# Residual vector quantizer: three index searches a unit over up to seven score tiles, in place of five

## The chip, the cores and the metric

One Trainium2 chip, one core of it. The metric is the device time of the whole kernel in microseconds (us): before the change 1495.66, the median of three runs (1492.65 to 1497.45).

## The reference

Four blocks run one after the other on x of shape (16, 32, 32, 32), each adding its result to x: a residual vector quantizer (L0), a frequency-domain attention block (L1), a directional scan network (L2) and a deformable convolution (L3). The change is in L0 alone:

```python
def _L0_conv_ref(embeddings, codebooks):      # 16384 pixels of 32 channels, 8 codebooks of 512 codes
    x = embeddings.transpose(0, 2, 3, 1).reshape(-1, e)
    def stage(res, cb):
        d = sum(res * res) - 2.0 * einsum('ne,ke->nk', res, cb) + sum(cb * cb)
        idx = argmin(d, axis=1)
        q = cb[idx]
        return (res - q, q)
    _, qs = scan(stage, x, codebooks)
    return sum(qs)
...
x = x + _L0_conv_ref(_gn(x), L0_conv_codebooks)
```

For every pixel and each of eight stages the nearest of 512 codes is found and subtracted from what is left of the pixel.

## The kernel before, in words

**Units.** `block_l0` holds the residual in SBUF as eight pieces `res[:, i, :]`, each of 128 partitions (4 images x 32 channels) by 512 pixels. One piece at one stage is a unit; eight stages make `ALL` = 64 units, in one software pipeline: unit w is scored in period w, its indices are turned into one-hot vectors in period w + 2, its codes are picked in w + 3, and so on (`back(w, n)` names the unit n periods back). A piece comes back for its next stage eight periods later.

**Tiles and slots.** A unit has 16 score tiles: 4 images (row groups of 32 partitions) by 4 runs of 128 pixels. A period has five slots of 4, 3, 4, 3, 2 tiles (even units) or 3, 4, 3, 4, 2 (odd ones), written out in `PLANS`. The slots use two areas of PSUM in turn (four banks and three). Before the change tile n is row group n // 4 and pixel run n % 4, and a slot takes every fourth number, so that its tiles lie in different row groups.

**Scores.** The codes are paired, so a tile's 512 columns are 256 sums and 256 differences. For a slot, TensorE makes the tiles (`scores`, L293 with the code norms and L298 in float32), ScalarE takes the relu of the difference half into `gain` (L423), and VectorE adds the sum half and the gain, scales by 4096 to the power of the tile's place, keeps the result in `scored` and its maximum in `top` (L669; each is followed in the trace by a read of the accumulator). TensorE may write slot k only when the tops of slot k - 2 are there, the area's last user.

**Search.** `find` (L637) looks up the positions of up to eight `top` values in the scored tiles of a slot. In the trace it is a load of the values (MATCH_VALUE_LOAD) and FIND_INDEX8. It stands one slot behind its scores, behind the pair sums of the next slot: the search of slot 0 behind slot 1, and so on, that of slot 4 behind slot 0 of the next unit. The low byte of a position is the pair's number in its tile.

**Order on VectorE** (`period`): slot 0, search of the last unit's slot 4; slot 1, transpose of the last unit's indices (`turn`, L646), search of slot 0; slot 2, the middle of the picked pair subtracted from the residual of unit w - 3 (`add_middle`, L652), search of slot 1; slot 3, search of slot 2; slot 4, search of slot 3. Ahead of each slot's pair sums stand two waits, each with a semaphore increment behind it: for the tops of the slot before, and for ScalarE's gain.

**Index rows.** SyncE writes the transposed indices to DRAM with one DMA (L238), waits for it, and reads them back, broadcast to all partitions, into `ib` (L243); it also loads each stage's codes and codebooks behind these (L220, L224, L225). GpSimd makes the near one-hots from `ib` (L515, four a unit), ScalarE the far ones in two steps (L398, L404).

**Picks.** TensorE multiplies the one-hots by the codebook (`pick`, L306): behind slots 0 and 1 the step, which ScalarE copies (L433), behind slots 2 and 3 the middle, which `add_middle` takes. Behind slot 4 comes one product matmul (L351), which waits for `add_middle` of the same period; ScalarE takes its sign (L449), and GpSimd updates the residual (L525, L535) and makes the next product (L543).

Of the kernel before, what the change touches and what calls it, by code (L numbers as in the profile page):

```python
# [46 lines left out]
    ((0, (0, 4, 8, 12)), (1, (1, 5, 9)), (0, (2, 6, 10, 14)), (1, (7, 11, 15)), (0, (3, 13))),  # L47
    ((1, (4, 8, 12)), (0, (1, 5, 9, 13)), (1, (2, 6, 10)), (0, (3, 7, 11, 15)), (1, (0, 14))),
)
SLOTS = 5  # L50
WIDE = 4
FOUND = 104
# [10 lines left out]
def block_l0(nc, ps, X, io, const, w1, next1):  # L63
# [14 lines left out]
    scratch = nc.dram_tensor("l0_indices", (2, TT, 2 * TILES, C), U16, kind="Internal").ap()  # L78
    with ExitStack() as ctx:
# [32 lines left out]
        scored = t("scored", [P, 3, WIDE * PAIRED])  # L112
        top = t("top", [P, 2, SLOTS, 8])
        idx = t("idx", [P, 2, FOUND], U16)
        turned = t("turned", [P, 2, 2 * TILES], U16)
        ib = t("ib", [P, 2, TT, TILES * C], U16)
# [5 lines left out]
        codes = scored[:, 0:1, :].rearrange("p o (s k) -> p (o s) k", k=K)  # L122
# [59 lines left out]
        def low(par, g, n):  # L182

            halves = ib[:, par].bitcast(U8).rearrange("p b (s c two) -> p s b c two", c=C, two=2)
            return halves[:, TT * g:TT * (g + n), :, :, 0]

        def spread(tile):

            return tile.rearrange("p (s b c) -> p s b c", b=TT, c=C)
# [12 lines left out]
        def _(sp):  # L202
# [30 lines left out]
            for v in range(ALL):  # L233
# [4 lines left out]
                sp.dma_start(scratch[par].rearrange("b s c -> (b s) c"), turned[:, par, :]).then_inc(s_wrote[par], 16)  # L238
                sp.wait_ge(s_wrote[par], START + 16 * (v // 2 + 1))
                if v >= 2:  # L240
# [3 lines left out]
                             scratch[par, :, 0:TILES, :].rearrange("b s c -> b (s c)").partition_broadcast(P)  # L244
# [17 lines left out]
        def _(pe):  # L262
# [18 lines left out]
            def scores(w, k):  # L281
# [9 lines left out]
                for m, n in enumerate(tiles):  # L291
                    rows = slice(C * (n // TT), C * (n // TT) + C)
                    pe.matmul(ps[:, at + m, :], row_slot[rows, par, :], csq[rows, :],  # L293
                              start=True, stop=False, skip_group_check=True)
                for m, n in enumerate(tiles):
                    rows = slice(C * (n // TT), C * (n // TT) + C)
                    tt = n % TT
# [62 lines left out]
        def _(act):  # L360
# [35 lines left out]
            def distance(v, g):  # L396

                nc.scalar.activation(spread(away[:, g:g + 2, :].rearrange("p g n -> p (g n)")), low(v % 2, g, 2),  # L398
# [156 lines left out]
        def _(dve):  # L555
# [74 lines left out]
            def find(w, k):  # L630

                area, tiles = PLANS[w % 2][k]
                at = (SLOTS * w + k) % 3
                if SLOTS * w + k:
                    dve.wait_ge(s_found, START + SLOTS * w + k)
                base, by = tiles[0], tiles[1] - tiles[0]
                nc.vector.max_index(idx[:, w % 2, base:base + 7 * by + 1:by],  # L637
                                    top[:, w % 2, k, :],
                                    scored[:, at, 0:len(tiles) * PAIRED]).then_inc(s_found, 1)

            def turn(v):

                dve.wait_ge(s_found, START + SLOTS * (v + 1))
                if v >= 2:
                    dve.wait_ge(s_wrote[v % 2], START + 16 * (v // 2))
# [8 lines left out]
            def period(w):  # L654

                early, mid = back(w, 1), back(w, 3)
                for k in range(SLOTS):
# [10 lines left out]
                    for m in range(len(tiles)):  # L668
                        nc.vector.tensor_tensor_reduce(  # L669
                            out=scored[:, (SLOTS * w + k) % 3, m * PAIRED:(m + 1) * PAIRED],  # L670
                            in0=ps[:, at + m, :PAIRED], in1=gain[:, at + m, :], scale=STEP_UP ** m, scalar=LOWEST,
                            op0=ALU.add, op1=ALU.max, accum_out=top[:, w % 2, k, m:m + 1]).then_inc(s_top, 1)
                    if k == 0 and early is not None:
                        find(early, SLOTS - 1)
                    if k == 1 and early is not None:
                        turn(early)
                    if k == 2 and mid is not None:
# [1536 lines left out]
```

## Time and profile before

| | before |
|---|---|
| median of three runs | 1495.66 us (1492.65 to 1497.45) |
| the profiled execution, its own time | 1497.99 us |
| its span, first to last instruction | 1495.9 us |
| busy over the span | PE 82%, DVE 78%, ACT 58%, POOL 64% |
| quantizer: first and last transposed indices | 41.1 us and 759.9 us |

PE is TensorE, DVE VectorE, ACT ScalarE, POOL GpSimd, SPq SyncE's DMA queue. In timeline rows the columns are the start from the span's start, the duration, the engine, the line of the kernel, the operation, output<-input and form, how many, and in brackets the engine's idle time before it and what ended it. An operation's row ends when its last result is written; the next one on the same engine can begin before that.

### The profile page before, as it was taken

Reading aid. Unit: us, or ns where it says so; the run is one execution under the profiler, and the core shown is the slowest. Engines: PE = TensorE matmul, PEld = TensorE weight load, DVE = VectorE, ACT = ScalarE, POOL = GpSimd, SP = SyncE. Lnnn points to the kernel's source line nnn. Section 1 sums busy time; section 2 is a strip of 40 time slices with the busy share of each in tenths; the row PEclk is TensorE's granted clock in tenths of the full one; section 3 lists DMA queues with packets and bytes.
Section 4 is the critical chain, followed back from the end, with each engine's and each line's share of the span. In section 5 each row is a group of like instructions: output and inputs, shape, how many; then the busy total and the mean of one; then the engine's idle time right before and its main releaser. Section 6 shows DMA issues by size and latency. Waiting matters only on the chain. (4 is left out here: it accounts for less than half of the span.)

```text
span 1495.9 us, 30285 instructions
## 1 busy us (share of the span) xinstructions
PE 1229.4 (82%) x10814; PEld 505.9 (34%) x10814; DVE 1170.9 (78%) x3667; ACT 871.4 (58%) x1169; POOL 954.5 (64%) x727
## 2 busy tenths in 40 slices
PE   4798988988988988988968899958888667776675
PEld 1222222222222222222215666626656411121111
DVE  6999999999999999999976455562222358887886
ACT  2687888888888888888843444320000046676654
POOL 5699888888888898898820332321000059989885
PEclk7799999999999999999979999989999959889877
DMA  7111211111121111111104433410000030202001
GB/s 175 52 44 44 68 46 55 45 52 60 45 68 45 53 48 57 55 44 58 44 30 101 106 89 86 103 41 18 2 1 2 23 73 1 48 1 62 1 15 29
DMA packets 65894, 74.43 MB, mean 50 GB/s; under 512 B 17776, under 2 KB 55920, under 8 KB 65744
## 3 DMA queue, kind: packets, MB, share of 16 engines
q1 hardware_dynamic: 64544, 70.68, 17.3%
q10 hardware_dynamic: 1200, 1.82, 0.5%
q8 instruction: 86, 1.41, 0.4%
q14 instruction: 64, 0.52, 0.1%
HBM read 42.21 MB, written 2.62 MB: 30 GB/s over the span
## 5 line engine op out<-in xcount | busy, mean ns | idle before, releaser
L515 POOL TENSOR_SCALAR l_onehot<-l_ib,c_cols 128x512 bf16<-128x512 uint8 x248 | 385.1, 1565 | 9.6 <-DMA l_ib<-l_indices 9.6
L669 DVE CUSTOM_DVE_ANT_0 l_scored<-ps,l_gain 128x256 f32<-128x256 f32 x1024 | 373.5, 416 | 14.2 <-ACT l_gain L423 13.4
L423 ACT ACTIVATE l_gain<-ps 128x1024 f32<-128x1024 f32 (+1 forms) x320 | 272.6, 852 | 144.9 <-PE ps L298 144.8
L298 PE MATMUL ps<-l_ct_slot,l_res 32*128 32x512 f32 x2048 | 340.1, 607 | 0.0
L637 DVE FIND_INDEX8 l_idx<-l_top,l_scored 128x8 uint16<-128x1024 f32 (+1 forms) x320 | 326.4, 1020 | 0.0
L1896 POOL TENSOR_TENSOR l_isum<-l_term 128x512 f32<-128x512 f32 x160 | 204.8, 1311 | 40.2 <-DVE l_term L2000 25.9
L306 PE MATMUL ps<-l_onehot,l_cbp_slot 128*32 128x512 bf16 x3072 | 217.1, 391 | 5.9 <-ACT l_signed L449 3.1
L293 PE MATMUL ps<-l_csq,l_row_slot 32*128 32x512 bf16 x1024 | 128.7, 394 | 84.0 <-DVE l_top L669 78.8
L1626 PE MATMUL ps<-l_isum,w_l_w_dsc 64*64 64x512 f32 x640 | 104.4, 713 | 59.8 <-POOL l_isum L1896 58.8
L1816 ACT ACTIVATE ps<-ps,w_l_minus 128x512 f32<-128x512 f32 x192 | 118.6, 661 | 51.2 <-DVE l_term L2006 35.1
L398 ACT ACTIVATE l_away<-l_ib,c_cols 128x1024 f16<-128x1024 uint8 x126 | 143.8, 1141 | 0.4 <-DMA l_ib<-l_indices 0.4
L404 ACT ACTIVATE l_onehot<-l_away,c_cols 128x1024 bf16<-128x1024 f16 x126 | 143.6, 1139 | 0.1
L306 PEld LDWEIGHTS ps<-l_onehot,l_cbp_slot 128*32 128x32 bf16 x3072 | 60.0, 96 | 230.2 <-issue 147.5
L298 PEld LDWEIGHTS ps<-l_ct_slot,l_res 32*128 32x128 f32 x2048 | 130.2, 191 | 7.4 <-issue 0.7
L2006 DVE SCALAR_TENSOR_TENSOR l_term<-ps,l_bend 128x512 f32<-128x512 f32 x192 | 120.7, 681 | 14.4 <-ACT ps L1816 12.8
L293 PEld LDWEIGHTS ps<-l_csq,l_row_slot 32*128 32x128 bf16 x1024 | 33.3, 91 | 263.7 <-DVE l_top L669 155.6
L1863 POOL COPY l_xe<-l_xe 128x128 f32<-128x128 f32 (+1 forms) x16 | 4.5, 308 | 183.9 <-DVE l_xe L1913 183.6
L525 POOL TENSOR_TENSOR l_signed<-l_signed,l_step 128x512 f32<-128x512 f32 x59 | 75.4, 1277 | 68.7 <-ACT l_signed L449 67.9
L2000 DVE SCALAR_TENSOR_TENSOR l_term<-ps,l_down 128x512 f32<-128x512 f32 x128 | 80.1, 680 | 26.0 <-PE ps L1618 15.8
L943 PE MATMUL ps<-l_wc,l_xi 128*128 128x192 f32 x512 | 93.0, 335 | 0.3 <-ACT l_qkv L1031 0.3
L943 PEld LDWEIGHTS ps<-l_wc,l_xi 128*128 128x128 f32 x512 | 83.6, 192 | 25.8 <-issue 17.1
L543 POOL TENSOR_TENSOR l_product<-l_res,l_step 128x512 f32<-128x512 f32 x61 | 77.8, 1275 | 12.6 <-DVE l_res L652 12.6
(214 smaller groups left out, 1604.3 us busy)
## 6 DMA issues: line engine op xcount, KB each, us to landing
l_ib<-l_indices SPq DMA_DIRECT2D x64, 512.0 KB, 3.7
l_xi<-l_xt SPq DMA_DIRECT2D x120, 128.0 KB
l_xi<-l_xz SPq DMA_DIRECT2D x36, 144.2 KB, 3.1
X<-in_x SPq DMA_DIRECT2D x16, 128.0 KB, 6.6
out<-X SPq DMA_DIRECT2D x16, 128.0 KB, 2.2
l_xr<-l_xt SPq DMA_DIRECT2D x30, 64.0 KB
l_ct<-in_codes_t SPq DMA_DIRECT2D x4, 448.0 KB, 12.1
l_ct_slot<-l_ct SPq DMA_DIRECT2D x7, 256.0 KB, 3.7
```

The costliest lines, as they stand in the source:

```text
L293: pe.matmul(ps[:, at + m, :], row_slot[rows, par, :], csq[rows, :], start=True, stop=False, skip_group_check=True)
L298: pe.matmul(ps[:, at + m, :], res[rows, i, P * tt:P * (tt + 1)], ct_slot[rows, par, :], start=False, stop=True, skip_group_check=True).the ...
L306: mm = pe.matmul(ps[C * g:C * g + C, PICK, :], cbp_slot[:, v // UNITS % 2, kind, a, c, :], onehot[:, v % 2, g, c, :], start=(c == 0 and a ...
L398: nc.scalar.activation(spread(away[:, g:g + 2, :].rearrange("p g n -> p (g n)")), low(v % 2, g, 2), ACT.Abs, bias=minus_iota[:, 1:2]).then ...
L404: nc.scalar.activation(onehot[:, v % 2, g:g + 2, 1, :], away[:, g:g + 2, :], ACT.Relu, bias=one[:], scale=-1.0).then_inc(s_far, 1)
L423: nc.scalar.activation(gain[:, at:at + len(tiles), :], ps[:, at:at + len(tiles), PAIRED:], ACT.Relu).then_inc(s_gain, 1)
L515: nc.gpsimd.tensor_scalar(spread(onehot[:, v % 2, g, 0, :]), low(v % 2, g, 1), iota[:, 0:1], None, ALU.is_equal).then_inc(s_near, 1)
L637: nc.vector.max_index(idx[:, w % 2, base:base + 7 * by + 1:by], top[:, w % 2, k, :], scored[:, at, 0:len(tiles) * PAIRED]).then_inc(s_foun ...
L669: nc.vector.tensor_tensor_reduce(out=scored[:, (SLOTS * w + k) % 3, m * PAIRED:(m + 1) * PAIRED], in0=ps[:, at + m, :PAIRED], in1=gain[:, ...
L943: pe.matmul(ps[:, CONV_BANKS[py % 2] + u, 0:HID], xi[:, n, g, at:at + P], wc[:, n, :], start=(n == 0), stop=False)
L1896: nc.gpsimd.tensor_tensor(isum[:, it % SUMS, :], term[:, t0, :], term[:, t0 + 1, :], ALU.add).then_inc(s_sum, 1)
L2006: nc.vector.scalar_tensor_tensor(out=dst, in0=grid(ps[:, RAMP + (p * NR + RAMP_OF[2 * n + e]) % RAMPS, :]), scalar=1.0, in1=bend[:, j % 2, ...
```

## The change

The tiles are numbered pixel run by pixel run, row group fastest (tile n is now row group n % 4 and pixel run n // 4), and a slot takes consecutive numbers. A search now covers the tiles of two slots: tiles 0 to 6, 7 to 13, and 14 and 15. `scored` gets a place for each of the three, `top` likewise. On VectorE the search of tiles 0 to 6 stands behind the pair sums of slot 2 and ahead of `add_middle`, that of tiles 7 to 13 behind slot 4, that of 14 and 15 behind slot 0 of the next unit. Behind slot 1 stands the transpose alone, behind slot 3 nothing. The DRAM rows of the indices are laid out so that a broadcast read is one run of 4 KB for each partition; to get there the transposed indices are written by four DMAs of 16 partitions.

```diff
--- before.py
+++ after.py
@@ -44,12 +44,12 @@
 SPAN = 2 * (2 / 1024 + 1 / 8192)
 
 PLANS = (
-    ((0, (0, 4, 8, 12)), (1, (1, 5, 9)), (0, (2, 6, 10, 14)), (1, (7, 11, 15)), (0, (3, 13))),
-    ((1, (4, 8, 12)), (0, (1, 5, 9, 13)), (1, (2, 6, 10)), (0, (3, 7, 11, 15)), (1, (0, 14))),
+    ((0, (0, 1, 2, 3)), (1, (4, 5, 6)), (0, (7, 8, 9, 10)), (1, (11, 12, 13)), (0, (14, 15))),
+    ((1, (0, 1, 2)), (0, (3, 4, 5, 6)), (1, (7, 8, 9)), (0, (10, 11, 12, 13)), (1, (14, 15))),
 )
 SLOTS = 5
-WIDE = 4
-FOUND = 104
+WIDE = 7
+SEARCHES = 3
 END = [[sum(len(plan[m][1]) for m in range(k + 1)) for k in range(SLOTS)] for plan in PLANS]
 KEPT = 4
 DRAIN = 5
@@ -75,7 +75,7 @@
     iota, eps = const["iota"], const["eps"]
     minus_iota, one, block_ones = const["minus_iota"], const["one"], const["block_ones"]
     part_mask, kept_rows, shift_row = const["part_mask"], const["kept_rows"], const["shift_row"]
-    scratch = nc.dram_tensor("l0_indices", (2, TT, 2 * TILES, C), U16, kind="Internal").ap()
+    scratch = nc.dram_tensor("l0_indices", (2, TILES, TT, C), U16, kind="Internal").ap()
     with ExitStack() as ctx:
         def t(name, shape, dt=F32):
             return ctx.enter_context(nc.sbuf_tensor("l0_" + name, shape, dt))
@@ -109,17 +109,17 @@
         cbp = t("cbp", [P, NC, 2, PARTS, CHUNKS, C], BF16)
         cbp_slot = t("cbp_slot", [P, 2, 2, PARTS, CHUNKS, C], BF16)
         gain = t("gain", [P, PICK, PAIRED])
-        scored = t("scored", [P, 3, WIDE * PAIRED])
-        top = t("top", [P, 2, SLOTS, 8])
-        idx = t("idx", [P, 2, FOUND], U16)
+        scored = t("scored", [P, SEARCHES, WIDE * PAIRED])
+        top = t("top", [P, 2, SEARCHES, 8])
+        idx = t("idx", [P, 2, 2 * TILES], U16)
         turned = t("turned", [P, 2, 2 * TILES], U16)
-        ib = t("ib", [P, 2, TT, TILES * C], U16)
+        ib = t("ib", [P, 2, TILES * P], U16)
         away = t("away", [P, G, HALF], F16)
         onehot = t("onehot", [P, 2, G, CHUNKS, HALF], BF16)
         step = t("step", [P, KEPT, HALF])
         product = t("product", [P, 2, HALF])
         signed = t("signed", [P, HALF])
-        codes = scored[:, 0:1, :].rearrange("p o (s k) -> p (o s) k", k=K)
+        codes = scored[:, 0, 0:2 * K].rearrange("p (s k) -> p s k", k=K)
 
         s_x = [sem(f"x{j}") for j in range(J)]
         s_codes = sem("codes")
@@ -181,12 +181,12 @@
 
         def low(par, g, n):
 
-            halves = ib[:, par].bitcast(U8).rearrange("p b (s c two) -> p s b c two", c=C, two=2)
-            return halves[:, TT * g:TT * (g + n), :, :, 0]
+            halves = ib[:, par].bitcast(U8).rearrange("p (t g n two) -> p g t n two", g=G, n=P, two=2)
+            return halves[:, g:g + n, :, :, 0] if n > 1 else halves[:, g, :, :, 0]
 
         def spread(tile):
 
-            return tile.rearrange("p (s b c) -> p s b c", b=TT, c=C)
+            return tile.rearrange("p (t n) -> p t n", n=P)
 
         def ib_ready(v):
 
@@ -235,13 +235,14 @@
                 sp.wait_ge(s_turned, START + v + 1)
                 if v >= 2:
                     sp.wait_ge(s_ib[par], ib_ready(v - 2))
-                sp.dma_start(scratch[par].rearrange("b s c -> (b s) c"), turned[:, par, :]).then_inc(s_wrote[par], 16)
-                sp.wait_ge(s_wrote[par], START + 16 * (v // 2 + 1))
+                for b in range(TT):
+                    sp.dma_start(scratch[par, :, b, :], turned[C * b:C * b + TILES, par, :]).then_inc(s_wrote[par], 16)
+                sp.wait_ge(s_wrote[par], START + 16 * TT * (v // 2 + 1))
                 if v >= 2:
                     sp.wait_ge(s_near, START + G * (v - 1))
                     sp.wait_ge(s_far, far_ready(v - 2))
                 sp.dma_start(ib[:, par],
-                             scratch[par, :, 0:TILES, :].rearrange("b s c -> b (s c)").partition_broadcast(P)
+                             scratch[par].rearrange("s b c -> (s b c)").partition_broadcast(P)
                              ).then_inc(s_ib[par], 16)
                 if v % UNITS == 1 and stage < NC:
                     sp.wait_ge(s_diff, START + 2 * stage)
@@ -289,12 +290,12 @@
                 elif w:
                     pe.wait_ge(s_top, START + (w - 1) * TILES + END[(w - 1) % 2][k + SLOTS - 2])
                 for m, n in enumerate(tiles):
-                    rows = slice(C * (n // TT), C * (n // TT) + C)
+                    rows = slice(C * (n % G), C * (n % G) + C)
                     pe.matmul(ps[:, at + m, :], row_slot[rows, par, :], csq[rows, :],
                               start=True, stop=False, skip_group_check=True)
                 for m, n in enumerate(tiles):
-                    rows = slice(C * (n // TT), C * (n // TT) + C)
-                    tt = n % TT
+                    rows = slice(C * (n % G), C * (n % G) + C)
+                    tt = n // G
                     pe.matmul(ps[:, at + m, :], res[rows, i, P * tt:P * (tt + 1)],
                               ct_slot[rows, par, :],
                               start=False, stop=True, skip_group_check=True).then_inc(s_score, 1)
@@ -627,22 +628,19 @@
             dve.wait_ge(s_clear, START + 2)
             dve.wait_ge(s_sums, START + 1)
 
-            def find(w, k):
-
-                area, tiles = PLANS[w % 2][k]
-                at = (SLOTS * w + k) % 3
-                if SLOTS * w + k:
-                    dve.wait_ge(s_found, START + SLOTS * w + k)
-                base, by = tiles[0], tiles[1] - tiles[0]
-                nc.vector.max_index(idx[:, w % 2, base:base + 7 * by + 1:by],
-                                    top[:, w % 2, k, :],
-                                    scored[:, at, 0:len(tiles) * PAIRED]).then_inc(s_found, 1)
+            def find(w, n):
+
+                first, last = WIDE * n, min(WIDE * (n + 1), TILES)
+                if SEARCHES * w + n:
+                    dve.wait_ge(s_found, START + SEARCHES * w + n)
+                nc.vector.max_index(idx[:, w % 2, first:first + 8], top[:, w % 2, n, :],
+                                    scored[:, n, 0:(last - first) * PAIRED]).then_inc(s_found, 1)
 
             def turn(v):
 
-                dve.wait_ge(s_found, START + SLOTS * (v + 1))
+                dve.wait_ge(s_found, START + SEARCHES * (v + 1))
                 if v >= 2:
-                    dve.wait_ge(s_wrote[v % 2], START + 16 * (v // 2))
+                    dve.wait_ge(s_wrote[v % 2], START + 16 * TT * (v // 2))
                 nc.vector.transpose(turned[:, v % 2, :], idx[:, v % 2, 0:2 * TILES]).then_inc(s_turned, 1)
 
             def add_middle(v):
@@ -665,19 +663,22 @@
                         dve.sem_inc(s_alone, 1)
                     dve.wait_ge(s_gain, START + w * SLOTS + (k + 1))
                     dve.sem_inc(s_alone, 1)
-                    for m in range(len(tiles)):
+                    for m, n in enumerate(tiles):
+                        search, place = divmod(n, WIDE)
                         nc.vector.tensor_tensor_reduce(
-                            out=scored[:, (SLOTS * w + k) % 3, m * PAIRED:(m + 1) * PAIRED],
-                            in0=ps[:, at + m, :PAIRED], in1=gain[:, at + m, :], scale=STEP_UP ** m, scalar=LOWEST,
-                            op0=ALU.add, op1=ALU.max, accum_out=top[:, w % 2, k, m:m + 1]).then_inc(s_top, 1)
+                            out=scored[:, search, place * PAIRED:(place + 1) * PAIRED],
+                            in0=ps[:, at + m, :PAIRED], in1=gain[:, at + m, :], scale=STEP_UP ** place, scalar=LOWEST,
+                            op0=ALU.add, op1=ALU.max, accum_out=top[:, w % 2, search, place:place + 1]).then_inc(s_top, 1)
                     if k == 0 and early is not None:
-                        find(early, SLOTS - 1)
+                        find(early, 2)
                     if k == 1 and early is not None:
                         turn(early)
+                    if k == 2:
+                        find(w, 0)
                     if k == 2 and mid is not None:
                         add_middle(mid)
-                    if k:
-                        find(w, k - 1)
+                    if k == 4:
+                        find(w, 1)
                     if w < 2:
                         late_quarters(w, k)
 
@@ -725,7 +726,7 @@
                 if early is not None:
                     dve.wait_ge(s_top, START + early * TILES + TILES)
                     dve.sem_inc(s_alone, 1)
-                    find(early, SLOTS - 1)
+                    find(early, 2)
                     turn(early)
                 if i == 0:
                     for e in range(UNITS - DRAIN):
```

## Rows read from the trace of the kernel before

**Rows 1.** Busy time by stretch: us, each engine's busy time (instructions), TensorE's granted clock, DMA.

```profile
0.00:100.00 100.00, 71.04 (x481) 23.04 (x481) 82.86 (x294) 55.55 (x77) 65.29 (x67) 0.80 0.37 96
418.58:429.70 11.12, 10.21 (x100) 3.27 (x98) 11.12 (x45) 9.28 (x12) 9.18 (x8) 1.00 0.26 76
429.70:441.27 11.57, 10.23 (x105) 3.27 (x98) 11.33 (x46) 9.34 (x12) 10.71 (x8) 1.00 0.21 57
```

**Rows 2.** The page's groups by line: busy us, mean ns | idle before, what ended it.

```profile
L669 DVE CUSTOM_DVE_ANT_0 l_scored<-ps,l_gain 128x256 f32<-128x256 f32 x1024 | 373.5, 416 | 14.2 <-ACT l_gain L423 13.4
```

**Rows 3.** Timeline of VectorE, an even unit (four tiles in slot 0).

```profile
418.58 0.42 DVE L669 CUSTOM_DVE_ANT_0 l_scored<-ps,l_gain 128x256 f32<-128x256 f32 x1
...
419.96 0.08 DVE L669 DVE_READ_ACCUMULATOR2_ANT l_top<- 128x1 f32 x1
419.96 0.09 DVE L637 MATCH_VALUE_LOAD l_idx<-l_top,l_scored 128x8 f32 x1
...
420.64 0.40 DVE L669 CUSTOM_DVE_ANT_0 l_scored<-ps,l_gain 128x256 f32<-128x256 f32 x1
...
422.96 0.41 DVE L669 CUSTOM_DVE_ANT_0 l_scored<-ps,l_gain 128x256 f32<-128x256 f32 x1
...
424.32 0.68 DVE L652 TENSOR_TENSOR l_res<-l_res,ps 128x512 f32<-128x512 f32 x1
...
425.86 0.40 DVE L669 CUSTOM_DVE_ANT_0 l_scored<-ps,l_gain 128x256 f32<-128x256 f32 x1
...
426.88 0.08 DVE L637 MATCH_VALUE_LOAD l_idx<-l_top,l_scored 128x8 f32 x1
...
428.09 0.40 DVE L669 CUSTOM_DVE_ANT_0 l_scored<-ps,l_gain 128x256 f32<-128x256 f32 x1
```

**Rows 4.** Timeline of VectorE, the odd unit behind it, to the next one's start.

```profile
429.70 0.40 DVE L669 CUSTOM_DVE_ANT_0 l_scored<-ps,l_gain 128x256 f32<-128x256 f32 x1
...
431.67 0.42 DVE L669 CUSTOM_DVE_ANT_0 l_scored<-ps,l_gain 128x256 f32<-128x256 f32 x1 [0.16 <-ACT l_gain L423]
...
434.09 0.40 DVE L669 CUSTOM_DVE_ANT_0 l_scored<-ps,l_gain 128x256 f32<-128x256 f32 x1
...
441.27 0.42 DVE L669 CUSTOM_DVE_ANT_0 l_scored<-ps,l_gain 128x256 f32<-128x256 f32 x1
```

**Rows 5.** Timeline of TensorE, the same two units.

```profile
420.10 0.39 PE L293 MATMUL ps<-l_csq,l_row_slot 32*128 32x512 bf16 x4 [0.16 <-DVE l_top L669]
...
425.64 1.12 PE L351 MATMUL ps<-l_product,c_block_ones 128*128 128x512 f32 x2
427.10 0.39 PE L293 MATMUL ps<-l_csq,l_row_slot 32*128 32x512 bf16 x3 [0.34 <-DVE l_top L669]
...
431.00 0.39 PE L293 MATMUL ps<-l_csq,l_row_slot 32*128 32x512 bf16 x3
```

**Rows 6.** Timeline of ScalarE, the same two units.

```profile
421.50 1.02 ACT L423 ACTIVATE l_gain<-ps 128x1024 f32<-128x1024 f32 x1 [0.90 <-PE ps L298]
...
430.46 1.02 ACT L423 ACTIVATE l_gain<-ps 128x1024 f32<-128x1024 f32 x1 [0.15 <-PE ps L298]
...
432.36 0.81 ACT L423 ACTIVATE l_gain<-ps 128x768 f32<-128x768 f32 x1 [0.41 <-PE ps L298]
```

**Rows 7.** Timeline of VectorE in the first unit, a slot behind a short instruction.

```profile
35.23 0.42 DVE L669 CUSTOM_DVE_ANT_0 l_scored<-ps,l_gain 128x256 f32<-128x256 f32 x1 [0.33 <-DVE l_rstd L569]
```

**Rows 8.** Timeline of SyncE's DMA issues, the same units.

```profile
421.89 0.32 SPq L238 DMA_DIRECT2D l_indices<-l_turned  x1
423.30 0.37 SPq L243 DMA_DIRECT2D l_ib<-l_indices  x1
423.76 0.47 SPq L224 DMA_DIRECT2D l_ct_slot<-l_ct  x1
```

**Rows 9.** The page's DMA issues: KB each, median us to landing.

```profile
l_ib<-l_indices SPq DMA_DIRECT2D x64, 512.0 KB, 3.7
```

**Rows 10.** Timeline of GpSimd, the odd unit's first near one-hot.

```profile
429.43 1.57 POOL L515 TENSOR_SCALAR l_onehot<-l_ib,c_cols 128x512 bf16<-128x512 uint8 x1
```

More of the change, by code:

```diff
@@ L396, in distance @@
             def distance(v, g):
-                nc.scalar.activation(spread(away[:, g:g + 2, :].rearrange("p g n -> p (g n)")), low(v % 2, g, 2),
+                nc.scalar.activation(away[:, g:g + 2, :].rearrange("p g (t n) -> p g t n", n=P), low(v % 2, g, 2),
                                      ACT.Abs, bias=minus_iota[:, 1:2]).then_inc(s_away, 1)
```

## The prediction

> **What bounds the kernel now.** I read the busy time by stretch first. Two successive units of the quantizer, taken at 418.58 us, last 11.12 and 11.57 us, 22.69 together, and VectorE is busy for 22.45 of them; TensorE has 20.44, GpSimd 19.89 and ScalarE 18.62 [rows 1]. So VectorE is the bound here. The groups by line say the same: before 1024 pair sums VectorE sat idle for only 14.2 us, nearly all of it until a relu of ScalarE was done [rows 2]. An edit on VectorE therefore counts at full price, as long as the next scores are ready when VectorE gets to them. That second half is what the timelines are for. I call the moments at which slots 0 to 4 of a unit start on VectorE T0 to T4.
>
> In the first unit shown (an even one: four tiles in slot 0) they are 418.58, 420.64, 422.96, 425.86 and 428.09 [rows 3]; the next unit starts at 429.70, with its T1 at 431.67, T2 at 434.09 and its end at 441.27 [rows 4]. Out of these come the unit prices. A pair sum takes 0.345 (four from 418.58 to 419.96), and its top stands 0.08 after the last. A search with its load takes 0.68 over 512 elements (419.96 to 420.64) and 1.21 over 1024 (426.88 to 428.09) [rows 3]: 0.265 per 256 elements and 0.15 that does not grow with them.
>
> **Term 1, the searches.** Five a unit (1024, 1024, 768, 768, 512) become three (1792, 1792, 512). The 4096 elements stay. By the line above 768 costs 0.945 and 1792 costs 1.21 + 3 x 0.265 = 2.00. Before: 2 x 1.21 + 2 x 0.945 + 0.68 = 4.99; after 4.68. Gain 0.31 a unit. No search of 1792 is in the trace; from slope errors of 0.01 it lies between 1.96 and 2.04.
>
> **Term 2, the handover of slot 2.** The two PSUM areas are used in turn, so the scores of slot k wait for the tops of slot k - 2. From T0 on, TensorE starts the four tiles of slot 2 1.52 later (420.10) [rows 5], ScalarE ends their relu 2.42 after that (421.50 + 1.02) [rows 6], and the shortest way from a relu's end to VectorE's start is 0.19 (430.46 + 1.02 = 431.48 to 431.67) [rows 4, 6]. So T2 cannot come before T0 + 4.13. It came at + 4.38: the cover was 0.25. That cover was the search of slot 0, 1.21 long, which stood behind slot 1. The change takes it away and puts its successor behind slot 2. VectorE is then free at T0 + 3.2 and waits: T2 = T0 + 4.13. Moving a search does not only move its cost, it uncovers a wait.
>
> **Term 3, VectorE waits for itself.** Before slot 4 there is no longer any work between the last pair sum of slot 3 and the wait for its top. Each such wait is followed by a semaphore increment, another wait and another increment. The nearest row is a slot that had to wait for a short VectorE instruction: 0.33 of idle time [rows 7]. I take 0.33 behind the last top, so 0.41 with the 0.08; the other bound is 0. In odd units slot 1's four tops also meet this wait, behind the transpose. A page of the Trainium skill speaks for the 0 (VectorE: DVE Perf Modes, The DRAIN you can't avoid): eight copies took the same time with a semaphore after each as with one at the end. By that the sum would be 1519; the row of this kernel shows 0.33 and decides my value.
>
> **The walk.** Even unit, from 418.58. T1 stays 420.64. T2 = 422.71. T3: before, 2.90 with a search of 0.945; now 2.90 - 0.945 + 2.00 = 3.955, so 426.67. T4: 2.23 - 1.21 + 0.41 = 1.43, so 428.10. End: 1.61 - 0.945 + 2.00 = 2.665, so 430.77 against 429.70. The middle's add now starts at 422.71 + 1.36 + 2.00 = 426.07 and ends 0.68 later at 426.75 (its 1.36 and 0.68 from [rows 3]). TensorE's product matmul waits for it, takes 1.12 [rows 5], and the next unit's scores start behind it at about 427.95. Their data would be ready by 430.3, so the end stands at 430.77 with some 0.4 of cover: this is where the later add would bite next.
>
> Odd unit. T1: VectorE is free at 430.77 + 1.03 + 0.68 = 432.48; TensorE's own path needs 4.57 from the first scores (427.10 to 431.67 [rows 4, 5]), so 427.95 + 4.57 = 432.52. T2: four pair sums and the wait for itself, 432.52 + 1.38 + 0.41 = 434.31; the three tiles' handover ends at about the same time (TensorE free at 431.9, then 2.17 from 431.00 to 432.36 + 0.81, then 0.19 [rows 5, 6]: 434.26). T3: 1.02 + 2.00 + 0.60 = 3.62, so 437.93. T4: 1.36 + 0.41, so 439.70. End: 2.665, so 442.37 against 441.27.
>
> A pair of units takes 23.79 instead of 22.69: 1.10 more, 0.55 a unit. There are 64; counting 62 for fill and drain gives **+34 us**. The profiled execution took 1497.99 (span 1495.9), so 1532.1 for such a run; it lies 2.3 above the median of the runs shown, 1495.66, so against that median 1529.8. With 0 for term 3 the same walk gives 23.44 a pair, +23 us and 1519.
>
> **What I cost at nothing.** The new order of tiles keeps four different row groups in a slot of four, so the scores should stay side by side. Four writes of index rows instead of one: a write is issued in about 0.46 (423.30 to 423.76) and the read followed the write by 1.41 [rows 8]; the read lands 3.7 later, at 427.0 [rows 9], and GpSimd takes it up at 429.43 [rows 10]. Three more issues put that 1.4 later, inside the 2.4 of cover, and the longer unit adds to it. SP's next loads of codes and codebooks stand behind the same three issues and are wanted a unit later. If the cover were gone, GpSimd's one-hots would be late for the picks. GpSimd and ScalarE read the indices in fewer, longer runs; they are not the bound, so a gain there is worth nothing. In the first units TensorE's granted clock was lower (0.80 on average over the first 100 us against 1.00 in the units above [rows 1]); the slot 2 wait is longer there, a few us in all.
>
> **Rivals.**
> 1. *VectorE stays the bound and only the searches count* (not slower). For it: VectorE is busy 99% of the two units, and the searches have a cost of 0.15 each that does not grow. Gain 0.31 and some 0.06 of former waits a unit, 62 times: -23 us, **1473**. It decides if the path from TensorE's start to VectorE's start of slot 2, 2.61 by the rows, is below 1.7. Against it: every piece of that path is a measured duration and none is edited. Chance 0.13.
> 2. *Half-way*: the search over 1792 costs less than the line says. Each 0.1 less saves 0.2 a unit; 0.28 less and nothing is left, **about 1497**. Against it: the two steps of 256 elements cost the same. Chance 0.07.
> 3. *The index rows come late.* The four writes run one behind the other. By this kernel's 1.41 each they take 5.6, and rows land some 0.4 us into the next unit, 0.7 later than GpSimd asks for them; its 9.95 of work in a unit of 11.9 leaves 1.95 to absorb that. From some 2.5 us more (an estimate) it decides: the one-hots then miss the picks of slot 0, and since the way from one unit's indices to those picks spans two units, half of each further us is lost a unit. With 0.5 too much, +16 on top: **1546**. [...] Here one write took 1.41, and no row shows four in flight. Chance 0.05.
>
> **Numbers.** The forecast keeps 0.75. Under 0.3% (4.5 us) a measurement of this kernel cannot tell from no change. Faster by more: rival 1, 0.13. Within: 0.07. Slower: 0.80, the forecast and rival 3. The forecast's own bounds are 1516 (term 3 at 0, search 1.96) to 1536 (search 2.04, startup). The range reaches to both sides until at most 2 in 10 is out: down to 1502, up to 1546.
>
> **What would show it.** Slot 2 of even units starts with 0.7 to 1.0 us of idle time on VectorE that the trace puts down to the relu; a second, 0.2 to 0.4 long, stands before slot 4; a pair of units lasts 23.4 to 23.9; the search over 1792 reads about 2.03 long. VectorE's share falls to about 95% in this part, and everything behind the quantizer keeps its length. No idle time at slot 2 would mean that I am wrong and rival 1 right; GpSimd waiting for index rows would mean rival 3.

## The result, and the profile after

The changed kernel takes 1533.84 us (median of four runs, 1531.51 to 1537.49) against 1495.41 for the kernel before: the ratio on record is 1.0251, interval 1.0229 to 1.0273. The forecast was 1529.8 us in a range from 1502 to 1546, and slower with a chance of 0.80.

| | before | after |
|---|---|---|
| the profiled execution, its own time | 1497.99 us | 1531.51 us |
| its span | 1495.9 us | 1529.1 us |
| first to last transposed indices | 718.7 us | 757.7 us |
| from there to the end | 736.0 us | 730.1 us |

Lines of the code moved by one or two: the pair sums are L668 now, the search L636, the relu L424, the add of the middle L650, the product matmul L352, the index write L239 and its read L244.

Busy time by stretch of the changed kernel, an even unit and the odd one behind it (us, then busy time of PE, PEld, DVE, ACT and POOL, granted clock, DMA share, GB/s); it answers to [rows 1]:

```profile
363.73:375.94 12.21, 10.20 (x101) 3.24 (x98) 11.06 (x42) 9.38 (x12) 9.60 (x8) 1.00 0.12 45
375.94:387.55 11.61, 10.26 (x102) 3.28 (x98) 11.09 (x41) 9.43 (x12) 10.28 (x8) 1.00 0.14 46
```

A pair lasts 23.82 where it lasted 22.69. VectorE's busy time fell from 22.45 to 22.15, and it now sits idle for 1.67 us of the pair where it was 0.24. (The searches alone save 0.58 a pair, as shown below. The busy time falls by less, because a row overlaps the next by some 0.08 where no wait stands between them, and there are now four waits.) The other engines have the same work as before. Nothing was added to any of them; the time is waiting.

The timeline of VectorE over the same two units shows where; it answers to [rows 3, 4]:

```profile
363.73 0.41 DVE L668 CUSTOM_DVE_ANT_0 l_scored<-ps,l_gain 128x256 f32<-128x256 f32 x1
...
365.17 0.69 DVE L636 FIND_INDEX8 l_idx<-l_top,l_scored 128x8 uint16<-128x512 f32 x1
365.77 0.41 DVE L668 CUSTOM_DVE_ANT_0 l_scored<-ps,l_gain 128x256 f32<-128x256 f32 x1
...
366.79 0.21 DVE L644 STREAM_TRANSPOSE l_turned<-l_idx 128x32 uint16<-128x32 uint16 x1
367.85 0.42 DVE L668 CUSTOM_DVE_ANT_0 l_scored<-ps,l_gain 128x256 f32<-128x256 f32 x1 [0.85 <-ACT l_gain L424]
...
369.30 2.02 DVE L636 FIND_INDEX8 l_idx<-l_top,l_scored 128x8 uint16<-128x1792 f32 x1
371.24 0.67 DVE L650 TENSOR_TENSOR l_res<-l_res,ps 128x512 f32<-128x512 f32 x1
371.82 0.42 DVE L668 CUSTOM_DVE_ANT_0 l_scored<-ps,l_gain 128x256 f32<-128x256 f32 x1
...
373.24 0.42 DVE L668 CUSTOM_DVE_ANT_0 l_scored<-ps,l_gain 128x256 f32<-128x256 f32 x1 [0.30 <-DVE l_top L668]
...
375.94 0.41 DVE L668 CUSTOM_DVE_ANT_0 l_scored<-ps,l_gain 128x256 f32<-128x256 f32 x1
...
379.46 0.42 DVE L668 CUSTOM_DVE_ANT_0 l_scored<-ps,l_gain 128x256 f32<-128x256 f32 x1 [0.22 <-ACT l_gain L424]
...
384.85 0.42 DVE L668 CUSTOM_DVE_ANT_0 l_scored<-ps,l_gain 128x256 f32<-128x256 f32 x1 [0.30 <-DVE l_top L668]
```

Read it slot by slot. Behind slot 0 stands the short search, behind slot 1 the transpose alone, and then VectorE waits 0.85 us for the relu of slot 2's scores. Before slot 4 it waits 0.30 for its own last top, in both units. Slot 2 of the odd unit waits 0.22, by the trace for the relu.

The timeline of TensorE in the even unit:

```profile
365.23 0.40 PE L294 MATMUL ps<-l_csq,l_row_slot 32*128 32x512 bf16 x4 [0.40 <-DVE l_top L668]
...
369.60 1.02 PE L299 MATMUL ps<-l_ct_slot,l_res 32*128 32x512 f32 x4
372.05 1.10 PE L352 MATMUL ps<-l_product,c_block_ones 128*128 128x512 f32 x2 [1.43 <-DVE l_res L650]
373.08 0.39 PE L294 MATMUL ps<-l_csq,l_row_slot 32*128 32x512 bf16 x3
```

Slot 2's scores start at 365.23, as soon as slot 0's tops are there, and VectorE starts slot 2 at 367.85: 2.62, the same handover as before (2.61 from [rows 4, 5, 6]). And TensorE now idles 1.43 us before the product matmul, which waits for the later add. That did not lengthen this unit, but it comes back below.

### The profile page after: what moved, and what is told of

It is laid out like the page before. It is cut to its first block and busy times, and to the rows that moved or that the text cites. A ratio compares the mean times of both kernels' runs of the same rounds, so it can differ in the third digit from the quotient of the medians.

```text
span 1529.1 us, 30202 instructions
## 1 busy us (share of the span) xinstructions
PE 1218.9 (80%) x10795; PEld 505.3 (33%) x10814; DVE 1161.5 (76%) x3411; ACT 876.8 (57%) x1169; POOL 954.1 (62%) x727
## 5 line engine op out<-in xcount | busy, mean ns | idle before, releaser
L668 DVE CUSTOM_DVE_ANT_0 l_scored<-ps,l_gain 128x256 f32<-128x256 f32 x1024 | 376.7, 419 | 64.5 <-ACT l_gain L424 43.6
L424 ACT ACTIVATE l_gain<-ps 128x1024 f32<-128x1024 f32 (+1 forms) x320 | 271.9, 850 | 142.0 <-PE ps L299 137.8
L636 DVE FIND_INDEX8 l_idx<-l_top,l_scored 128x8 uint16<-128x1792 f32 (+1 forms) x192 | 302.5, 1576 | 0.0
L352 PE MATMUL ps<-l_product,c_block_ones 128*128 128x512 f32 x128 | 73.0, 653 | 80.2 <-DVE l_res L650 79.3
```

Source lines behind the costliest of these rows:

```text
L424: nc.scalar.activation(gain[:, at:at + len(tiles), :], ps[:, at:at + len(tiles), PAIRED:], ACT.Relu).then_inc(s_gain, 1)
L636: nc.vector.max_index(idx[:, w % 2, first:first + 8], top[:, w % 2, n, :], scored[:, n, 0:(last - first) * PAIRED]).then_inc(s_found, 1)
L668: nc.vector.tensor_tensor_reduce(out=scored[:, search, place * PAIRED:(place + 1) * PAIRED], in0=ps[:, at + m, :PAIRED], in1=gain[:, at + ...
```

## The experiments

Each ran on one chip beside the kernel before; its ratio is against those runs. Where units are given below, they are the time from one unit's transpose to the next one's: 11.29 and 11.40 in the kernel before, 11.58 and 12.24 in the changed one. Such a unit holds parts of an even and of an odd one, so the two numbers are not those of the stretches above; their sum is the same pair. Each profile is of one execution. The first five experiments ask which part of the change costs the time.

**1. The new layout alone.** The changed kernel with five searches again, one slot behind their scores:

```diff
-SEARCHES = 3
+SEARCHES = 5
...
-                    if k == 2:
-                        find(w, 0)
...
-                    if k == 4:
-                        find(w, 1)
+                    if k:
+                        find(w, k - 1)
```

> The changed kernel with five searches again, each one slot behind its scores as before; the new numbering of the tiles, the new layout of the index rows and the four DMA writes stay. My theory (the lost search between slots 1 and 2 and the waits of VectorE for itself make the loss): everything else in the change costs nothing, so 1495 us, within 5 of the kernel before, and a pair of units lasts 22.7 us. The rival that the rows or the layout cost the time: close to 1534, with GpSimd or ScalarE waiting for index rows.

Measured: 1494.19 us, 0.999 (0.997 to 1.0011), and units of 11.29 and 11.40 as before. The numbering of the tiles, the rows' layout, the four writes and the relative order of everything else cost nothing. The loss lies in the searches and where they stand.

**2. One write of index rows in the changed kernel.**

```diff
...
-                for b in range(TT):
-                    sp.dma_start(scratch[par, :, b, :], turned[C * b:C * b + TILES, par, :]).then_inc(s_wrote[par], 16)
...
+                sp.dma_start(scratch[par].rearrange("s b c -> b s c"), turned[:, par, :]).then_inc(s_wrote[par], 16)
...
```

> The changed kernel with one DMA for the index rows in place of four (the unused rows go along to their own place in DRAM; the read stays one run of 4 KB). Theory: the rows land earlier, nobody had waited for them, so 1534, within 4. Rival (four small writes cost time): 1500 to 1525.

The rows that hold no index go along, and `scratch` is twice as large for them.

Measured: 1530.83 us, 1.0232 (1.0198 to 1.0267), against 1.0251 (1.0229 to 1.0273) with four: no difference that these intervals resolve. SyncE's timeline in the changed kernel shows why four writes are no burden:

```profile
367.02 1.69 SPq L239 DMA_DIRECT2D l_indices<-l_turned  x4
369.72 0.34 SPq L244 DMA_DIRECT2D l_ib<-l_indices  x1
```

The read follows the first write by 2.70 where it was 1.41 [rows 8]: 1.3 later, 1.4 forecast. Four writes one behind the other, at 1.41 each, would have taken 5.6: the writes are in flight together.

**3. The cover put back.** The search of tiles 0 to 6 behind slot 1's transpose:

```diff
-                    if k == 2:
+                    if k == 1:
+                        dve.wait_ge(s_top, START + w * TILES + END[w % 2][1])
                         find(w, 0)
```

> The changed kernel with the search of tiles 0 to 6 moved from behind slot 2 to behind the transpose of slot 1, with a wait for its tops. Theory: the 0.9 us of idle time before slot 2 of even units goes, and slot 2 starts 5.2 us after the unit's start by the work in front of it. But the work between slots 2 and 4 is now only the add and slot 3, so a new wait for scores of about 0.6 stands before slot 4. A pair of units 23.3 instead of 23.8, time about 1520. Rival (the search is merely long and the place does not matter): 1534 unchanged.

Measured: 1530.47 us, 1.025 (1.0217 to 1.0284); not the 1520 expected. Most units last 11.27 and 12.08, 23.35 together as expected, and the idle time moved as expected. No slot 2 is idle any more. The rows with idle time in some two units of VectorE's timeline are a slot 1 of an odd unit that waits for its scores, slot 4 of the same unit that waits for its own top, and slot 4 of the even unit behind it, with the new wait for scores:

```profile
401.23 0.42 DVE L668 CUSTOM_DVE_ANT_0 l_scored<-ps,l_gain 128x256 f32<-128x256 f32 x1 [0.47 <-ACT l_gain L424]
...
408.12 0.42 DVE L668 CUSTOM_DVE_ANT_0 l_scored<-ps,l_gain 128x256 f32<-128x256 f32 x1 [0.30 <-DVE l_top L668]
...
419.62 0.42 DVE L668 CUSTOM_DVE_ANT_0 l_scored<-ps,l_gain 128x256 f32<-128x256 f32 x1 [0.53 <-ACT l_gain L424]
```

But about one in three of the long units lasts 13.45 instead of 12.08, ten in all, which makes some 14 us. TensorE's granted clock was at its lower level for 34 us of the quantizer in this profile. That needed an experiment of its own (6 and 7).

**4. The add first.** The middle's add ahead of the search again, everything else as changed:

```diff
-                    if k == 2:
-                        find(w, 0)
                     if k == 2 and mid is not None:
                         add_middle(mid)
+                    if k == 2:
+                        find(w, 0)
```

> The changed kernel with the add of the middle ahead of the search of tiles 0 to 6, as the order was before. Theory: the add then waits for TensorE's last middle pick, which stands behind the scores of slot 3; VectorE sits idle there for 0.8 to 1 us in units of both kinds, so a pair of units lasts 24.6 and the time is about 1560. So the move of the add is a part of the change that pays. Rival (the later add delays the product matmul and through it the next unit's scores, so that undoing it gains): under 1530.

Measured: 1611.12 us, 1.079 (1.0756 to 1.0824); some 50 above the 1560 expected. In stretches with the clock up a pair lasts 24.6, as expected (12.33 and 12.27), though not in the way expected: the add waits for TensorE's last pick in odd units only, 0.66 us in this row of VectorE's timeline. In even units, where slot 2 has waited 0.85 for its relu already, it does not wait:

```profile
170.63 0.69 DVE L650 TENSOR_TENSOR l_res<-l_res,ps 128x512 f32<-128x512 f32 x1 [0.66 <-PE ps L307]
```

So the move of the add pays, 0.8 us a pair. The further 50 us go with the clock again: 147 us at the lower level, and from the middle on pairs of 27.3. No experiment fills TensorE's idle time in this kernel, so that this is all of it is not shown.

**5. The waits moved to the searches.** No slot waits for the last slot's tops, each search waits for its own:

```diff
+                dve.sem_inc(s_alone, 1)
+                dve.wait_ge(s_top, START + w * TILES + last)
                 nc.vector.max_index(idx[:, w % 2, first:first + 8], top[:, w % 2, n, :],
...
-                    if k == 0 and early is not None:
-                        dve.wait_ge(s_top, START + early * TILES + TILES)
-                        dve.sem_inc(s_alone, 1)
-                    if k:
-                        dve.wait_ge(s_top, START + w * TILES + END[w % 2][k - 1])
-                        dve.sem_inc(s_alone, 1)
```

> The changed kernel without the wait for the last slot's tops ahead of each slot; each search waits for its own tops instead. Theory: the idle time of 0.3 before slot 4 goes in every unit. It is won fully in even units, in odd units part of it is given back at slot 1, which waits for its scores. A pair of units 23.4 instead of 23.8, time about 1522. Rival (a semaphore between VectorE instructions costs nothing, as a page of the Trainium skill has it): 1534 unchanged.

Measured: 1558.82 us, 1.0417 (1.0378 to 1.0455). Both expectations missed: the kernel became slower than the changed one. The pairs with the clock up did shrink, to 11.22 and 12.25, 23.47 together, 23.4 expected. But of every three long units one lasts 15.3 and one 13.8, and the clock was low for 95 us.

**6. TensorE's idle time filled.** Experiment 5, with four matmuls of 512 columns behind slot 4's scores, into a bank that nobody reads then. Their results are not used:

```diff
+FILL = 4
...
+                    if k == SLOTS - 1 and w < ALL and late is not None:
+                        area, tiles = PLANS[w % 2][k]
+                        spare = AREAS[area][0] + len(tiles)
+                        for _ in range(FILL):
+                            pe.matmul(ps[:, spare, :], row_slot[:, stage % 2, :], csq[:], start=True, stop=True,
+                                      skip_group_check=True)
```

> The kernel whose waits stand at the searches, plus four matmuls of 512 columns behind the scores of slot 4, into a PSUM bank that nobody reads then; they add no result and fill about 0.9 of the 2 us in which TensorE waits for the add. Theory: that kernel read 1559 instead of the 1522 expected, because TensorE's granted clock fell to its lower level for 96 us of the quantizer, and it fell because TensorE sat idle. With the gap partly filled it stays up, and what remains is the walk: a pair of units 23.5, time 1515 to 1525. Rival (the falls come from elsewhere, or the pair of units is longer for another reason): 1559 or more.

Measured: 1513.55 us, 1.0132 (1.01 to 1.0163), 1.5 below the 1515 to 1525 expected. More work on TensorE, and 45 us less. Busy time by stretch from 100 to 700 us, first without the filling (experiment 5), where the clock stands at 0.93:

```profile
100.00:700.00 600.00, 525.58 (x4715) 164.25 (x4716) 533.72 (x1925) 452.24 (x530) 484.49 (x344) 0.93 0.15 48
```

and with it, at 1.00:

```profile
100.00:700.00 600.00, 567.05 (x5215) 181.77 (x5211) 565.53 (x2041) 480.60 (x562) 515.13 (x366) 1.00 0.15 50
```

Nearly all units last 11.22 and 12.24, and from the fourth on none is over 12.4.

**7. The same filling in the changed kernel.**

> The changed kernel with the same four filling matmuls behind the scores of slot 4. Theory: the changed kernel's profile has TensorE at the lower clock for 10 us of the quantizer, which cost 5.3 us in two units; filled, it stays up, the pair of units stays at 23.8, time 1526 to 1530. Rival (the filling itself delays the scores of the next unit): a pair over 23.9 and 1534 or more.

Measured: 1528.8 us, 1.0208 (1.0185 to 1.0231), and its profile has units of 11.58 and 12.24 with no lower clock between the 85th us and the last transpose. The filling does not delay anything here: the pair is as long as without it. The gain against 1.0251 is small and the intervals just touch.

**8. The same filling in experiment 3.**

> The kernel with the search of tiles 0 to 6 behind slot 1, plus the four filling matmuls. Theory: its undisturbed pairs lasted 23.35, and the way from there to the measured 1530 was the clock, 34 us at the lower level in its profile; filled, 1513 to 1520. If the gap in which TensorE idles there is another one than the filled one, the clock still falls and 1530 stays.

Measured: 1545.77 us, 1.0329 (1.0305 to 1.0352): worse than without it, outside both expectations. The timeline of TensorE shows that the idle time lies ahead of slot 4's scores there, and the filling (L349) stands behind them, in the way of the next unit's scores. First experiment 3, then the same with the filling:

```profile
417.51 0.39 PE L294 MATMUL ps<-l_csq,l_row_slot 32*128 32x512 bf16 x2 [1.23 <-DVE l_top L668]
...
418.69 1.12 PE L352 MATMUL ps<-l_product,c_block_ones 128*128 128x512 f32 x2
419.75 0.39 PE L294 MATMUL ps<-l_csq,l_row_slot 32*128 32x512 bf16 x3
```

```profile
402.78 0.39 PE L295 MATMUL ps<-l_csq,l_row_slot 32*128 32x512 bf16 x2 [1.23 <-DVE l_top L675]
...
404.19 0.81 PE L349 MATMUL ps<-l_csq,l_row_slot 128*128 128x512 bf16 x3 [0.16 <-issue]
404.84 1.02 PE L359 MATMUL ps<-l_product,c_block_ones 128*128 128x512 f32 x2
405.79 0.39 PE L295 MATMUL ps<-l_csq,l_row_slot 32*128 32x512 bf16 x3
```

From slot 4's scores to the next unit's it is 3.01 where it was 2.24. The clock stayed up but for 3.4 us; the units became 11.99 and 12.59. Filling is no cure in itself: behind the gap it held the clock up here and cost more than that gave, in the gap (experiments 6 and 7) it cost nothing.

**9. Other groups.** Three searches, over slot 0, slots 1 and 2, and slots 3 and 4, at the changed kernel's places, with experiment 5's waits:

```diff
+GROUP = (0, 1, 1, 2, 2)
+RANGES = [[(end[0] - len(plan[0][1]), end[0]), (end[0], end[2]), (end[2], end[4])] for plan, end in zip(PLANS, END)]
...
-                first, last = WIDE * n, min(WIDE * (n + 1), TILES)
+                first, last = RANGES[w % 2][n]
...
-                        search, place = divmod(n, WIDE)
+                        search = GROUP[k]
+                        place = n - RANGES[w % 2][search][0]
```

> Three searches again, but over other slots: slot 0 alone, slots 1 and 2, slots 3 and 4, at the same places on VectorE as in the changed kernel (behind slot 2, behind slot 4, behind slot 0 of the next unit), and each search waits for its own tops instead of each slot for those of the last. Theory: the search behind slot 0 now covers 5 or 6 tiles and takes 1.5 to 1.7 us, so slot 2's scores are ready in time; no wait stands before slot 4. A pair of units takes 22.0 to 22.2 us against 22.69 before, so about 1476 us, under both kernels, and TensorE is so busy that its granted clock stays at its upper level. Rival (three searches a unit cost more than five by themselves): 1500 or more.

Measured: 1478.22 us, 0.9881 (0.9853 to 0.991), 1.2% faster than the kernel before. Units of 11.17 and 10.85. Its timeline of VectorE through slots 0 to 2 of an odd unit, and then of the even one behind it:

```profile
418.95 0.40 DVE L667 CUSTOM_DVE_ANT_0 l_scored<-ps,l_gain 128x256 f32<-128x256 f32 x1
...
420.04 1.49 DVE L640 FIND_INDEX8 l_idx<-l_top,l_scored 128x8 uint16<-128x1280 f32 x1
421.75 0.42 DVE L667 CUSTOM_DVE_ANT_0 l_scored<-ps,l_gain 128x256 f32<-128x256 f32 x1 [0.22 <-ACT l_gain L426]
...
423.14 0.21 DVE L648 STREAM_TRANSPOSE l_turned<-l_idx 128x32 uint16<-128x32 uint16 x1
423.27 0.38 DVE L667 CUSTOM_DVE_ANT_0 l_scored<-ps,l_gain 128x256 f32<-128x256 f32 x1
...
430.16 0.42 DVE L667 CUSTOM_DVE_ANT_0 l_scored<-ps,l_gain 128x256 f32<-128x256 f32 x1
...
431.62 1.75 DVE L640 FIND_INDEX8 l_idx<-l_top,l_scored 128x8 uint16<-128x1536 f32 x1
...
434.44 0.38 DVE L667 CUSTOM_DVE_ANT_0 l_scored<-ps,l_gain 128x256 f32<-128x256 f32 x1
```

The search behind slot 0 is 1.49 or 1.75 long instead of 0.69. In the odd unit slot 2 starts 0.13 behind the transpose's start. In the even unit, whose slot 2 had waited 0.85, it starts at +4.28, later than the +4.13 that the handover needs, and with no wait. The number of searches, their total length and the places are the changed kernel's, and the waits are experiment 5's; only which slots they cover differs.

**10. These groups with the changed kernel's waits.**

> The same three groups, but with the changed kernel's wait for the last slot's tops ahead of every slot. Theory: 0.3 to 0.4 us before slots 2 and 4 comes back, a pair of units takes 23.0, time about 1505, if the clock holds; more if it falls. Rival (own waits are free): the time of the kernel without them, 1476.

Measured: 1505.46 us, 1.007 (1.0044 to 1.0096), units of 11.53 and 11.53. The clock stayed up in the profiles of both. The waits for its own tops cost VectorE 27 us here by the two medians. Against the changed kernel, whose waits this one has, the grouping alone is worth 28 us (1505.46 against 1533.84).

**11. The control.** The kernel before, its waits moved to the searches:

> The kernel before with its waits for tops moved from the slots to the searches, nothing else. Theory: each of those waits was covered by the search that stood in front of it, so nothing changes, 1495 within 4; the gain of the regrouped kernel comes from the two searches fewer, not from this. Rival (the waits cost VectorE time there too): under 1488.

Measured: 1493.59 us, 0.998 (0.9965 to 0.9996), units of 11.29 and 11.40 as before. A gain of 0.2%, too small to matter: where a search stands in front of the wait, it costs nothing.

## Why the prediction was right

**The walk.** It gave an even unit of 12.19 and an odd one of 11.60, 23.79 together; the profile has 12.21 and 11.61, 23.82. Slots of the even unit were put at +2.06, +4.13, +8.09 and +9.52 and stand at +2.04, +4.12, +8.09 and +9.51. VectorE's share of this part was put at 95% and is 93%.

**Term 1.** The search over 1792 elements reads 2.02 long in the timeline, and load and search together take 2.01 from start to next start, 2.00 forecast. With 0.68 for the short one that makes 4.70 a unit instead of 4.99: 0.29 gained, 0.31 forecast, the saved fixed parts of two searches.

**Term 2.** The handover was forecast to place slot 2 at +4.13 and did. Experiment 9 shows the other half: with searches of the same number and sum, and a longer one behind slot 0, the wait is gone. Experiment 3 shows that putting the cover back at slot 2 uncovers slot 4: five gaps share two long searches, and which gap stays bare is what the grouping decides.

**Term 3.** 0.33 was taken, 0.30 measured before slot 4, in every unit. In slot 2 of the odd unit the walk had the wait for itself and the handover end within 0.05 of each other; by the trace it was the handover that ended last. With 0 for this term the walk gave 23.44 a pair, and experiment 5, without these waits, has 23.47. What it is worth was forecast as the step from 1519 to 1529.8, 11 us; experiments 6 and 7, which differ in these waits alone and both keep the clock, are 11 us apart by their ratios (0.0076 of 1495), 9.8 us in the profiles' quantizer (742.2 against 752.0), and 15 us by their medians, whose runs of the kernel before are 3 us apart too. In experiments 9 and 10 it is 27 us, where two slots a unit wait for themselves. The rule that I weighed against it (the Trainium skill, VectorE: DVE Perf Modes, The DRAIN you can't avoid: a semaphore after each of eight copies cost nothing extra) does not carry over to this wait: here a wait for a result, an increment, a second wait and a second increment stand between two instructions, and the trace shows 0.30 of idle time.

**What I costed at nothing** was nothing: experiments 1 and 2. The read of 4 KB runs still lands in 3.7 us. GpSimd waited for index rows once between the 100th and the 740th us, for 0.7 us. The first four intervals between transposes grew by 1.1 us in all, less than the walk alone gives for them (2.3), so the few us more that I had named for the lower clock there do not show. But up to the 85th us the clock was low for 41 us in the profile before and for 31 in the one after, so these two profiles do not settle it.

**The rest of the difference.** From first to last transpose the quantizer grew by 39.0 us, and 63 intervals at the pair's 0.565 each give 35.6. The first units took 1.1 us less than that. And the profile adds two stretches of lower clock that no step of mine contains, 4.6 us in two units (15.27 and 13.88, both instead of 12.24; the 5.3 in the expectation of experiment 7 compared the second with a short unit). Behind the quantizer 5.9 us came back. I had put that part at no change, and its code is the same; what differs is TensorE's clock, low there for 162 us in the profile before (0.89 on average) and for 129 in the one after (0.91):

```profile
759.86:1495.90 736.04, 565.96 (x4646) 293.26 (x4634) 436.16 (x822) 275.80 (x455) 307.57 (x249) 0.89 0.17 41
```

```profile
799.05:1529.10 730.05, 551.35 (x4627) 290.72 (x4638) 436.60 (x822) 275.86 (x455) 307.48 (x249) 0.91 0.17 42
```

So the mechanism was right, and the closeness of the total is in part luck. For a run like the profiled one I had forecast 1532.1, and it took 1531.51: the 4.6 us of lower clock in the quantizer and the 5.9 us that came back behind it, neither of them forecast, nearly cancel. By the medians the change costs 38 us where 34 were forecast.

**The rivals.** Rival 1 (only the searches count) fell with the 0.85 us of idle time; experiment 9, where the handovers are covered, comes near to it (1478 us, rival 1 had 1473). Rival 2 fell with the measured search. Rival 3 fell with experiment 2.

## What to carry to other kernels

When two engines hand buffers to each other in turn, the work from slot k to slot k + 2 is a cover, and it must be at least as long as slot k's own work and the handover behind it (here 1.5 us for four pair sums and 2.6 from TensorE's start to VectorE's). Merging two small instructions on the bound engine saves their fixed part (0.15 us each) but makes one long cover and one bare gap; so first list every gap with what will stand in it, then choose the groups. A wait for one's own last result was free where other work stood in front of it (experiment 11) and cost 0.30 us where none did.

## What the runs showed that I had not expected

TensorE's clock fell in the middle of the quantizer, and where it did the loss was larger than all terms of the walk. In the changed kernel's timeline of TensorE it looks like this:

```profile
410.70 1.02 PE L299 MATMUL ps<-l_ct_slot,l_res 32*128 32x512 f32 x6
...
417.25 1.02 PE L299 MATMUL ps<-l_ct_slot,l_res 32*128 32x512 f32 x4
419.70 2.05 PE L352 MATMUL ps<-l_product,c_block_ones 128*128 128x512 f32 x2 [1.44 <-DVE l_res L650]
421.68 0.61 PE L294 MATMUL ps<-l_csq,l_row_slot 32*128 32x512 bf16 x3
422.08 1.92 PE L299 MATMUL ps<-l_ct_slot,l_res 32*128 32x512 f32 x6
```

and by stretch, the 13.65 us before the fall and the 6.82 us of it:

```profile
405.66:419.31 13.65, 10.79 (x102) 3.28 (x98) 12.50 (x44) 11.01 (x14) 10.83 (x8) 1.00 0.19 60
419.31:426.13 6.82, 6.43 (x31) 2.13 (x35) 5.09 (x18) 3.20 (x4) 4.75 (x4) 0.50 0.12 38
```

TensorE had idled four times in the unit before, at last for 1.44 us while it waited for the add, and then worked at 1.2 GHz instead of 2.4: six matmuls of the scores took 1.92 us instead of 1.02. The time at the lower level between the 85th us and the last transpose, each from one profile, was 0 in the kernel before, 10 us in the changed one and in experiment 2, 34, 95 and 147 in experiments 3, 5 and 4, 3.4 in experiment 8, and 0 in experiments 1, 6, 7, 9, 10 and 11. Experiments 5 and 6 show that TensorE's idle time causes the fall: the same kernel with the gap partly filled did not fall in its profile, and all its runs lie 37 us or more below all of the other's. When exactly it falls stays open. The amount of idle time alone doesn't sort the kernels: with the clock up a unit has the same TensorE work of 10.2 us everywhere, in 11.9 us in the changed kernel, and in 11.7 in experiments 5 and 3, which idle less and fell more. The longest gap that comes back in every pair was 1.12 us or less in the seven profiles that did not fall and 1.23 to 2.02 us in the six that did, while single gaps of up to 1.5 us passed without a fall. The filling of experiment 6 cut it to 0.47, but added work as well, so a rule for its length is not shown. The changed kernel has its gap of 1.44 us in every pair, too, and fell for it once. An edit that shortens VectorE's work can thus lengthen the kernel, as in experiment 5, and a small edit here should be judged with the granted clock beside it.
